# A decoder's K/V/Q projection stage with seven half-size products in place of eight

## What is computed

```
u = (x - mean(x)) / sqrt(var(x) + 1e-5)
q = einsum('blh,dh->bdl', u, Wq) + bq
k = einsum('blh,dh->bdl', u, Wk) + bk
v = einsum('blh,dh->bdl', u, Wv) + bv
```

## Time and profile before

| | |
|---|---|
| time, median of 3 runs | 5498.76 us (5492.18 to 5499.02) |
| the profiled execution's own time | 5492.75 us |
| its span | 5491.0 us |
| TensorE busy in the span | 5175.9 us (94%) |
| mean granted TensorE clock | 0.975 |
| products of this stage, busy | 336.1 us in 768 records |
| the stage, from its first load of x (line 159) to the next stage's first matmul | 1874.38 to 2232.18 us |

### The profile page before, as it was taken

The page is one execution under the profiler, slowest core; times in us unless marked ns, Lnnn a source line. Parts: engine busy times, 40 slices in busy tenths (PEclk is TensorE's granted clock), DMA queues, the critical chain, the costliest instruction groups (busy, mean ns, idle before and its releaser), DMA issues. The chain is left out here.

```text
span 5491.0 us, 75665 instructions
## 1 busy us (share of the span) xinstructions
PE 5175.9 (94%) x25460; PEld 2561.9 (47%) x25460; DVE 2640.4 (48%) x4293; ACT 1644.5 (30%) x2110; POOL 1434.4 (26%) x1122
## 2 busy tenths in 40 slices
PE   9999989999999999899978999599999899999998
PEld 4444446644445444444444555444443344444444
DVE  4252237654343322355533665455555455555554
ACT  1011025522211100234321443134443344334443
POOL 1010015511112100000011222444444444444443
PEclk9999999999999999999999999699999999999999
DMA  1010021320012223799975113388778846756547
GB/s 57 8 54 0 16 77 51 96 79 16 21 35 73 98 92 124 167 220 214 221 206 189 39 62 120 109 303 279 249 270 282 282 113 195 264 159 208 185 139 250
DMA packets 492542, 771.55 MB, mean 141 GB/s; under 512 B 119154, under 2 KB 262262, under 8 KB 491844
## 3 DMA queue, kind: packets, MB, share of 16 engines
q1 hardware_dynamic: 376208, 723.32, 40.9%
q0 software_dynamic: 36160, 43.09, 4.1%
q10 hardware_dynamic: 79988, 2.67, 0.9%
HBM read 577.15 MB, written 116.26 MB: 126 GB/s over the span
## 5 line engine op out<-in xcount | busy, mean ns | idle before, releaser
L2938 PE MATMUL ex_ps<-ex_w,ex_xT 128*64 128x512 f32 x5248 | 1201.1, 600 | 66.3 <-DVE ex_w L2840 66.3
L2840 DVE COPY ex_w<-ex_shelf 128x4096 f32 x328 | 753.4, 2297 | 434.9 <-PE ex_ps L2938 244.1
L2889 ACT ACTIVATE ex_w<-ex_shelf 128x4096 f32 x164 | 593.3, 3618 | 865.9 <-PE ex_ps L2954 786.7
L2938 PEld LDWEIGHTS ex_ps<-ex_w,ex_xT 128*64 128x64 f32 x5248 | 366.0, 138 | 688.8 <-issue 595.8
L2954 PE MATMUL ex_ps<-ex_w,ex_hT 128*64 128x256 f32 x5248 | 597.8, 381 | 21.0 <-issue 17.2
L2786 POOL DMA_INDIRECT ex_x<-moe_xn,ex_ix x328 | 559.3, 1705 | 134.2 <-issue 98.8
L2803 POOL DMA_INDIRECT out<-ex_y,ex_ix_out x164 | 290.2, 1770 | 955.3 <-DVE ex_xT L2827 520.7
L2954 PEld LDWEIGHTS ex_ps<-ex_w,ex_hT 128*64 128x64 f32 x5248 | 382.5, 138 | 279.8 <-issue 114.3
L1561 PE MATMUL ff_ps<-ff_w,ff_hT 128*128 128x512 f32 x768 | 349.0, 597 | 6.5 <-DVE ff_y L1442 3.7
L1756 PE MATMUL pr_ps<-pr_w,pr_xT 128*128 128x512 f32 x768 | 336.1, 595 | 0.8 <-ACT pr_xT L225 0.8
L1510 ACT ACTIVATE ff_gT<-ff_ps,ff_bet,ff_gam 128x128 f32<-128x128 f32 x384 | 143.9, 459 | 459.1 <-PE ff_ps L1571 459.1
(11 more groups left out here) (277 smaller groups left out, 6799.6 us busy)
## 6 DMA issues: line engine op xcount, KB each, us to landing
ex_shelf<-L_ffn_w SPq DMA_DIRECT2D x128, 2048.0 KB
ex_shelf<-L_ffn_wo SPq DMA_DIRECT2D x64, 2048.0 KB
cv_gt<-cv_g SPq DMA_DIRECT2D x320, 128.0 KB, 3.3
cv_vt<-cv_v SPq DMA_DIRECT2D x256, 128.0 KB, 5.2
ff_x<-x SPq DMA_DIRECT2D x16, 1024.0 KB, 8.1
ex_raw_x<-slot_token ACTq DMA_DIRECT2D x656, 0.5 KB
at_low<-x SPq DMA_DIRECT2D x8, 1024.0 KB
x<-at_acc SPq DMA_DIRECT2D x8, 1024.0 KB, 4.2
```

The source lines that it names most:

```text
L2840: dve.tensor_copy(w_s[n][:, :], pick(shelf[n], buf)).then_inc(w_set[n].sem, 1)
L2889: act.activation(w_s[2][:, :], pick(shelf[2], buf), ACT.Copy).then_inc(w_set[2].sem, 1)
L2938: mm = pe.matmul(ps[q * G:(q + 1) * G, which, 0:FQ], xT[:, p % 2, k, :], wu[which][:, k, q * FQ:(q + 1) * FQ], start=k == 0, stop=k == KD - 1)
```

## The change

```diff
@@ open_project
-    st.w0 = st.sb("w0", [P, KD, D])
+    st.wl = st.sb("wl", [P, KD, 3 * D // 2])
     st.ident_in = st.sem("ident_in")
     st.x_in = [st.sem("x_in0"), st.sem("x_in1")]
-    st.w_in = [st.sem(f"w_in{i}") for i in range(len(ws))]
+    st.wl_in = st.sem("wl_in")
...
+        sp.dma_start(st.wl[:, :, 0:D], weight_view(ws[0])).then_inc(st.wl_in, 16)
+        sp.dma_start(st.wl[:, :, D:], weight_view(ws[1])[:, :, 0:D // 2]).then_inc(st.wl_in, 16)
     st.early = early
@@ stage_project
     M = len(ws)
+    WN = M * D
+    NH = WN // 2
+    NPC = NH // 2
+    HK = KD // 2
+    UC = 4
+    W = NC * UC
+    ident, ident_in, wl, wl_in = st.ident, st.ident_in, st.wl, st.wl_in
...
+        wh = st.sb("wh", [P, KD, NH])
+        bias = st.sb("bias", [P, WN])
+        t_s = st.sb("t", [P, 4, HK, NH])
+        s_s = st.sb("s", [P, 2, 4, HK, CH // 2])
         f = Front(st, ps, 6, x_in, x=[st.x0, st.sb("x1", [P, TJ, D])], x_in=st.x_in)
+        y = st.sb("y", [P, 2, TJ, WN])
+        wh_in = st.sem("wh_in")
+        bias_in = st.sem("bias_in")
+        t_done = st.sem("t_done")
+        s_done = st.sem("s_done")
+        p1_mm, p2_mm, p3_mm, p4_mm, p5_mm, p6_mm, p7_mm = (st.sem(f"p{i}_mm") for i in range(1, 8))
+        c11_set, c12_set, c22_set = st.sem("c11_set"), st.sem("c12_set"), st.sem("c22_set")
+        c11_done, c12_done, c21_done, c22_done = (st.sem(f"c{i}_done") for i in (11, 12, 21, 22))
         stored = [st.sem("stored0"), st.sem("stored1")]
         block = st.ctx.enter_context(nc.Block())
+        T1, T2, T3, T4 = range(4)
+        S1, S2, S4, S3 = range(4)
+        low = lambda n: slice(n * NPC, (n + 1) * NPC)
+        high = lambda n: slice(NH + n * NPC, NH + (n + 1) * NPC)
+        def unit(g):
+            return g // UC, g % UC // 2, g % 2
         @block.sync
         def _(sp):
             row = lambda v: v.rearrange("(o n) -> o n", o=1).to_broadcast([P, D])
             f.load(sp, 1, 1)
+            sp.dma_start(wh[:, :, 0:D // 2], weight_view(ws[1])[:, :, D // 2:]).then_inc(wh_in, 16)
+            sp.dma_start(wh[:, :, D // 2:], weight_view(ws[2])).then_inc(wh_in, 16)
+            for i in range(M):
+                sp.dma_start(bias[:, i * D:(i + 1) * D], row(biases[i])).then_inc(bias_in, 16)
             sp.wait_ge(st.tail, 16 * TJ)
             st.plain(sp)
+            for c in range(NC):
+                if c + 2 < NC:
                     sp.wait_ge(*f.xn_done(c))
+                    f.load(sp, c + 2, c % 2)
+                if c == NC - 2:
+                    sp.wait_ge(stored[0], 16 * 2 * M)
+                    sp.wait_ge(stored[1], 16 * 2 * M)
                     st.plain(sp)
                     nxt.early(sp)
+                for tb in range(2):
+                    for s in (c11_done, c12_done, c22_done, c21_done):
+                        sp.wait_ge(s, c * UC + 2 * tb + 2)
                         st.plain(sp)
+                    for i in range(M):
+                        sp.dma_start(chunk_rows(outs[i], c)[:, tb::2, :], y[:, c % 2, tb::2, i * D:(i + 1) * D]).then_inc(stored[c % 2], 16)
+            sp.wait_ge(stored[0], 16 * 2 * M * (NC // 2))
+            sp.wait_ge(stored[1], 16 * 2 * M * (NC // 2))
...
+            def combine(c):
+                p = c % 2
+                a11, a12 = f.xT[:, p, 0:HK, 0:CH // 2], f.xT[:, p, HK:KD, 0:CH // 2]
+                a21, a22 = f.xT[:, p, 0:HK, CH // 2:CH], f.xT[:, p, HK:KD, CH // 2:CH]
+                pool.wait_ge(*f.xT_done(c))
+                if c >= 2:
+                    pool.wait_ge(p7_mm, (c - 1) * UC)
+                pool.tensor_tensor(s_s[:, p, S1], a21, a22, ALU.add).then_inc(s_done, 1)
+                pool.wait_ge(s_done, 4 * c + 1)
+                pool.tensor_tensor(s_s[:, p, S2], s_s[:, p, S1], a11, ALU.subtract).then_inc(s_done, 1)
+                pool.wait_ge(s_done, 4 * c + 2)
+                pool.tensor_tensor(s_s[:, p, S4], a12, s_s[:, p, S2], ALU.subtract).then_inc(s_done, 1)
+                pool.wait_ge(s_done, 4 * c + 3)
+                pool.tensor_tensor(s_s[:, p, S3], a11, a21, ALU.subtract).then_inc(s_done, 1)
+            f.rstd(pool, 0, 0)
+            f.rstd(pool, 1, 1)
+            combine(0)
+            for c in range(NC):
+                if c + 2 < NC:
+                    f.rstd(pool, c + 2, c % 2)
+                if c + 1 < NC:
+                    combine(c + 1)
         @block.vector
...
+            def moments(c, j):
+                p = c % 2
+                if j == 0:
+                    dve.wait_ge(*f.x_ready(c, p))
+                    dve.wait_ge(*f.mv_done(c - 2))
+                dve.bn_stats(f.bn[:, p, j, :], f.x[p][:, j, :]).then_inc(f.bn_done.sem, 1)
+            def gather(c, j):
+                p = c % 2
+                if j == 0:
+                    dve.wait_ge(*f.var_done(c - 2))
+                    dve.wait_ge(*f.xn_done(c - 2))
+                dve.wait_ge(*f.bn_done(c, j + 1))
+                dve.bn_aggr(f.mv[:, p, j, :], f.bn[:, p, j, :]).then_inc(f.mv_done.sem, 1)
+            def ahead(c, slot):
+                if c >= NC:
+                    return
+                if slot < 4:
+                    moments(c, slot)
+                elif slot < 6:
+                    gather(c, 2 * slot - 8)
+                    gather(c, 2 * slot - 7)
+                elif 7 <= slot < 11:
+                    f.normalise_tile(dve, c, c % 2, slot - 7)
+            def c21(g):
+                c, tb, n = unit(g)
+                dve.wait_ge(p4_mm, g + 1)
+                dve.tensor_tensor(y[:, c % 2, tb + 2, low(n)], ps[:, g % 2, 0:NPC], bias[:, low(n)], ALU.add).then_inc(c21_done, 1)
+            def evict(g):
+                c, tb, n = unit(g)
+                p, q, slot = c % 2, g % 2, g % UC * 3
+                a, b, e = ps[:, q, 0:NPC], ps[:, 2 + q, 0:NPC], ps[:, 4 + q, 0:NPC]
+                y11, y12, y22 = y[:, p, tb, low(n)], y[:, p, tb, high(n)], y[:, p, tb + 2, high(n)]
+                if g % UC == 0 and c >= 2:
+                    dve.wait_ge(stored[p], 16 * 2 * M * (c // 2))
+                dve.wait_ge(p1_mm, g + 1)
+                dve.tensor_tensor(y11, a, bias[:, low(n)], ALU.add).then_inc(c11_set, 1)
+                if g:
+                    c21(g - 1)
+                ahead(c + 2, slot)
+                dve.wait_ge(p2_mm, g + 1)
+                dve.wait_ge(c11_set, g + 1)
+                dve.tensor_tensor(y11, b, y11, ALU.add).then_inc(c11_done, 1)
+                ahead(c + 2, slot + 1)
+                dve.wait_ge(p5_mm, g + 1)
+                dve.tensor_tensor(y22, e, bias[:, high(n)], ALU.add).then_inc(c22_set, 1)
+                dve.wait_ge(p6_mm, g + 1)
+                dve.tensor_tensor(y12, a, bias[:, high(n)], ALU.add).then_inc(c12_set, 1)
+                dve.wait_ge(p3_mm, g + 1)
+                dve.wait_ge(c12_set, g + 1)
+                dve.tensor_tensor(y12, e, y12, ALU.add).then_inc(c12_done, 1)
+                dve.wait_ge(p7_mm, g + 1)
+                dve.wait_ge(c22_set, g + 1)
+                dve.tensor_tensor(y22, a, y22, ALU.add).then_inc(c22_done, 1)
+                ahead(c + 2, slot + 2)
+            f.stats(dve, 0, 0)
+            f.normalise(dve, 0, 0)
+            dve.wait_ge(wl_in, 32)
+            dve.wait_ge(wh_in, 32)
+            b11, b12, b21, b22 = wl[:, 0:HK, :], wh[:, 0:HK, :], wl[:, HK:, :], wh[:, HK:, :]
+            dve.tensor_tensor(t_s[:, T1], b12, b11, ALU.subtract).then_inc(t_done, 1)
+            dve.wait_ge(t_done, 1)
+            dve.tensor_tensor(t_s[:, T2], b22, t_s[:, T1], ALU.subtract).then_inc(t_done, 1)
+            dve.tensor_tensor(t_s[:, T3], b22, b12, ALU.subtract).then_inc(t_done, 1)
+            dve.wait_ge(t_done, 2)
+            dve.tensor_tensor(t_s[:, T4], b21, t_s[:, T2], ALU.subtract).then_inc(t_done, 1)
+            f.stats(dve, 1, 1)
+            f.normalise(dve, 1, 1)
+            dve.wait_ge(bias_in, 16 * M)
+            dve.wait_ge(st.tail, 16 * TJ)
+            for g in range(W):
+                evict(g)
+            c21(W - 1)
...
+            f.keep(act, 0, 0, f.xT_done(-1))
+            for c in range(1, NC):
+                if c >= 2:
+                    act.wait_ge(p4_mm, (c - 1) * UC)
+                f.keep(act, c, c % 2, f.xT_done(c - 1))
...
+            def product(bank, lhs, rhs, first):
+                for k in range(HK):
+                    i = pe.matmul(bank[:, 0:NPC], lhs[:, k], rhs[:, k], start=first and k == 0, stop=k == HK - 1, skip_group_check=not first)
+                return i
+            def rows(c, tb, right, lower):
+                at = (tb + 2 * lower) * P
+                return f.xT[:, c % 2, HK * right:HK * right + HK, at:at + P]
+            def mixed(c, tb, s):
+                return s_s[:, c % 2, s, :, tb * P:(tb + 1) * P]
+            def p4(g):
+                c, tb, n = unit(g)
+                pe.wait_ge(c22_done, g + 1)
+                product(ps[:, g % 2], rows(c, tb, 1, 1), t_s[:, T4, :, low(n)], False).then_inc(p4_mm, 1)
```

(75 more changed lines are left out.)

6 lines of the change are left out of this document (removed).

## The result

The changed kernel takes 5530.56 us (median of 4 runs, 5525.05 to 5536.9), the kernel before 5495.48 us (4 runs, 5492.18 to 5499.02) in the same comparison: a ratio of 1.0064, 95% interval 1.0047 to 1.0082, so 35 us slower. The forecast was 5530. The profiled execution took 5525.05 us, with a span of 5523.1 us.

A forecast was written before the change was run, and what follows sets the result against it. TensorE's columns were taken to set the time. The terms -41.0 + 40.5 + 10 + 15 + 2 + 4.4 gave about +31 us, so 5530 us on the median, range 5504 to 5550.

The forecast's parts named there:

- products: TensorE's matmuls in the stage: 896 records of 384 columns replace 768 of 512, giving back 41.0 us.
- five stalls at P3: Chunks 1 to 5: TensorE stands 8.1 us at P3 while VectorE waits for x ahead of evictions; 40.5 us in all.
- clock behind them: TensorE at half clock after each of the five stalls: 2.0 us each, 10 us in all, bounds 0 and 12.5.
- start: Stage's start: T, statistics, and normalisations alternating with GpSimd's S delay P3; 15 us, bounds 7 and 18.
- GpSimd's S in later chunks: Slot 7's normalisation can wait out one S, leaving P3 late by up to 0.5 us: 6 chunks, 2 us (0 to 3).
- end: Stage's end: P7's eviction ahead of P4, then three stores of 0.5 MB in place of one of 256 KB; 4.4 us.
- VectorE late in every unit: Rival, 9%: seven chained evictions answer 0.5 us later than said, three places a unit lose some 0.2 each; 19 us, so 5549.
- x is there in time: Rival, 10%: loads land before TensorE uses up its 4.8 us, or stalls too short to lower the clock; -20, so 5479.

The follow-up runs named there:

- e1: Changed kernel with the load of x for chunk c+3 issued behind chunk c's first three stores, half a chunk earlier: 5455.51 us, 0.9964 of the kernel before.
- e2: Changed kernel with VectorE's work on the chunk ahead started two slots later, loads unmoved: 5456.09 us, 0.9965 of the kernel before.
- e4: Changed kernel with 60 idle transposes ahead of TensorE's c22_set wait in the first unit of chunks 1 to 5: 5494.38 us, 1.0040 of the kernel before.
- e5: Changed kernel with the stage's start reordered: chunk 1's statistics during the weights' wait, GpSimd's S only behind T4: 5504.05 us (one run), stage 372.52 us.
- e7: Changed kernel with the last half chunk stored tile by tile as evictions allow: 5503.68 us (one run), stage 373.20 us.
- e3: Changed kernel with the load of x issued ahead of the three stores at the same point of SP's list: 5490.42 us, 1.0028 of the kernel before.

## Why the prediction was right

The time, the sign and the mechanism came as forecast. Step by step, for the profiled executions:

| step | forecast | measured | from |
|---|---|---|---|
| products | -41.0 | -40.5 | a unit 9.03 us, 0.3225 us a record, x 896 |
| five stalls at P3 | +40.5 | +37.1 | waits of the changed kernel; e1, e2 |
| clock behind them | +10 | +13.0 | P3 and P7; e4 |
| start | +15 | +12.3 | 20.06 - 6.04 - 1.7; e5 |
| GpSimd's S in later chunks | +2 | 0 | |
| end | +4.4 | +4.4 | 3.6 behind the last eviction, 0.9 ahead of P4, 0.1 off; e7 |
| sum | +31 | +26.3 | stage: +27.1 |

**Products.** The width scaled as the 384-column form of another stage had said. Seven evictions in a chain hurt nowhere once x is there: in e1 TensorE waits for an eviction only in the first unit (1.1 us) and ahead of the last P4 (0.7). The rival "VectorE late in every unit" is out.

**The stall** was 7.4 in place of 8.1, mostly because VectorE waited 9.3 us for x and not 9.74. In chunk 1 P3 then started 2.27 us behind x in place of 2.36, and TensorE got there 4.15 us after c21 in place of 4.0. "x is there in time" was right in what it would bring: the early load gives it, and its 0.9964 is the -20 that I had worked out for it, though its stage is 23.5 us shorter: that -20 had the start and the later chunks 4.7 us too dear, as below. It was wrong only in that this kernel doesn't do it.

**The clock** was undersized: 2.6 us a stall, above the 2.5 seen in the earlier trace rows. I had taken 2.0, between the 1.7 and the 2.5 of two rows; here the half clock lasts for some 5 us behind each stall, and all of it falls on dense products.

**The start** was oversized by 2.7 us. T1 started when I had said, at 1885.79, but the first product came 1.6 us later than before, so T1 is 0.5 us behind it where I had 2.1; in the other runs whose start is the same it is 0.4 to 0.8. And the exclusion of VectorE and GpSimd cost 3.8 us (5.69 less 1.92), where I had let four pairs of 1.65 follow one another, 4.7.

**Later chunks.** A normalisation in slot 7 took 0.81 us in place of 0.54 (chunk 1, at 1970.90), and no product waited for it: the slot had room. The forecast's 2 us weren't there.

**What the sum doesn't hold.** The median moved by 35 us, the stage by 27. That the forecast of 5530 met the median to within 1 us is luck: it set out from a median of 5498.76, 3.3 us above the 5495.48 of this comparison, its stage was 4 us too dear, and 8 us of the measured difference lie outside the stage, where no step of mine puts anything. The executions of one kernel spread over 7 to 12 us here, so I leave those 8 open.

## What to carry to other kernels

Fewer products pay by the column, but only while every engine's answer comes within the cover that is left; before a restructuring, write down for each wait what stands behind it on its engine and who needs that, and how many products lie in between. A load that was issued late enough to be hidden by four banks stalls TensorE for most of its length behind a chain of one product (7.4 of 9.3 us); moving either its issue or the first instruction that waits for it gave back all of 50 us, and each was a change of a few lines. When a stall drops TensorE's clock it costs more than its length, here by a third (13.0 us on 37.1) to not quite a half (10.2 on 22.7), so count it in.

## What the runs showed of the hardware

- A stall of 4.3 to 4.7 us already dropped the clock to half: P3 and P7 behind it took 4.4 to 5.2 us, behind one of 7.3 to 7.6 us 5.0 to 5.3, in place of 2.58. It need not fall during the stall: in chunk 3 of e3 it was still 1.00 when P3 began, at 2040.68 after 4.57 us of waiting, and 0.53 in the window from 2041 on. With all but 0.8 to 1.4 us of each stall filled by idle transposes, P3 and P7 took 2.7 us.
- A load of 1 MB with nothing ahead of it in its queue took 6.2 us from issue to use, with its first microsecond at 86 GB/s while the DMA engines counted as 0.85 busy; a store of 1 MB landed in 4.3 in the kernel before. The load had three stores behind it; what it takes alone wasn't tried.
- Four GpSimd additions of 128 x 512 beside four normalisations on VectorE took 1.26, 1.33, 1.33 and 1.32 us, and the four normalisations 5.69 in place of 1.91. The Trainium skill, page "SBUF — State Buffer" (Who interferes with whom), says that the two shut each other out for whole instructions; moving GpSimd's additions behind brought 1.91 back.
